# Value groups and reciprocals moved up in the image steps, and another order of loads ahead of the first expert tile

## Chip, cores and metric

The kernel runs on one core of a Trainium2 chip. The metric is the device time of one execution, in microseconds (us). Every run of the comparison uses the same inputs.

## What is computed

One layer of a small vision tower, all in float32, on 16 images of 128 tokens with 256 channels each:

```python
h = tok_mixer(x)                      # x: (16, 4, 128, 256); softmax-weighted sum over the 4 groups
h = h + attention(layernorm(h))       # 16 heads of 16, bias from relative positions, then Wo
h = h + moe(layernorm(h))             # 8 experts, top 2 of a softmax gate, 256 -> 1024 -> 256, exact GELU

# moe, as the reference has it
gates = softmax(x @ Wg + bg); mask = one_hot(top_k(gates, 2)); g = normalise(gates * mask)
eo = gelu(x @ W1[e] + b1[e]) @ W2[e] + b2[e];  out = sum_e g[e] * eo[e]
```

The kernel computes only the two chosen experts of a token. It sorts the 4096 (token, expert) pairs into 39 tiles of up to 128 rows with one expert each. The first 14 tiles (EARLY) are filled from images 0 to 10 alone, so that they can start before the last images are routed.

## The kernel before, in words

Each engine has its own program, written out by hand. The engines meet only at semaphores, and each runs its own instructions strictly in the written order.

**Image stage.** Step i of every engine's `step` works on three images at once: the front part does projections and scores of image i, the back part softmax sums, transposes, values and context of image i-1, and the late part output projection, residual, second norm and gate logits of image i-2. Steps 0 to 15 have a front; step 16 has only back and late. Steps 6, 10 and 13 also have gate work on VectorE (`gate_inputs`, `masks`, `gates`); steps 7, 11 and 14 have `ranks` on TensorE and `rows` on VectorE, which fix where the token records go.

- TensorE (lines 873 to 911): `project_qk`, `context` 0 and 1 (transposes of the probabilities, line 815), `out_project`, `project_v`, then `values(0)`, `context(2)`, `values(1)`, `scores(0)`, `context(3)`, `spread_sums` (transposes of the reciprocals, line 771), `values(2)`, `scores(1)`, `values(3)`, `turn_xn2`, `scores(2)`, `turn_x`, `scores(3)`, `gate_logits`. A `values` group is eight small matmuls (line 825) that use 32 of the array's columns each.
- VectorE (lines 1227 to 1265): token mixing of the next image (`select_groups`), `mask_keys` (line 263), `residual`, `first_norm` (line 1089, writes `xn1`), `rows`, `reciprocals` (line 1132), `spread` (two copies, line 1137), `second_norm` (line 1089, writes `xn2`), `masks`, `biased` 0 and 1 (line 1122: score plus bias and row minimum), `normalise`, `biased` 2 and 3.
- ScalarE (lines 605 to 634): copies out of PSUM and the exponentials (line 586), 16 per step in four groups. `exp(i, 0)` waits for `biased(i, 0)`; the last copies of a step are `x1T_evac` (line 555), which lets TensorE begin the next step, and `v_evac`.
- GpSimd (lines 447 to 456): the power -1/2 of the first norm (line 428), its half of `mask_keys` (line 263), the power of the second norm (line 428), and the scatters of token records into DRAM (line 439). Of these, a scatter with an even number waits until all scatters before it have landed.

**Hand-over.** After step 14 VectorE makes the table of the early tiles (`tile_table`, semaphore `tables_ok`). SyncE, which issues nearly all plain DMAs through one queue, has in order: seven times `load_w2(e)` (1 MB of second-layer weights, which waits until the images that lie in its place are used up) with `store_xn2` of two images (normed tokens and residual, 128 KB each), then `load_w2(7)`, a store of a padding row block, `b2` (result biases, 1 MB, line 324, waits for the last `biased`), a wait for `tables_ok`, a wait for the 22 early scatters (`scat`, line 327), then per tile the token records (`load_records`, `next_records`: 2 KB) and the first-layer matrix (`load_w1`: 1 MB). `next_records(j)` waits until the records of tile j-1 have landed.

**Expert stage.** GpSimd gathers the 128 token rows of a tile through its records (`gather`, line 476) and later scatter-adds the results (`scatter`, line 485). TensorE turns the rows (`turn_xs`, line 932), VectorE copies them out (`xs_evac`, line 1343), TensorE computes `hidden` (line 944, 32 matmuls), ScalarE applies GELU (line 672), and TensorE computes `second` (line 956) one tile behind. VectorE's `result` (line 1348) adds `b2`. Between the first two tiles TensorE has `out_project(15)` and VectorE `residual(15)`; before `xs_evac(0)` VectorE waits for `b2_in`.

## Time and profile before

| | |
|---|---|
| median of 3 runs | 566.88 us (564.5 to 567.76) |
| the profiled execution | 565.29 us, of which its span is 563.5 us |
| TensorE matmuls busy | 510.7 us (91% of the span) |
| VectorE busy | 239.5 us (42%) |
| ScalarE busy | 265.3 us (47%) |
| GpSimd busy | 200.2 us (36%) |
| mean granted TensorE clock | 0.976 of full speed |
| last chain, by engine | PE 60%, DVE 10%, issue 10%, DMA 8%, ACT 6%, POOL 3% |

PE is TensorE, DVE VectorE, ACT ScalarE, POOL GpSimd, SP SyncE. A busy share is a mean over stages that have different limits. The chain of work that ended last is followed back from the last instruction, at each step to what released it; "issue" is time in which an engine waited for nothing that the profile shows. The time in square brackets behind an instruction is how long its engine had been idle, with what ended that.

### The profile page before, as it was taken

How to read it: one execution, taken by the hardware profiler on the slowest of the kernel's cores; microseconds unless marked ns; L12 is line 12 of the kernel's file. 1: busy time of each engine (PE TensorE's matmuls, PEld its weight loads, DVE VectorE, ACT ScalarE, POOL GpSimd, SP SyncE). 2: the span in 40 equal slices, each digit the busy share in tenths (PEclk: the TensorE clock that was granted, in tenths of full speed). 3: DMA queues.
4: the chain of work that ended last, by engine and by line, in shares of the span. 5: the costliest groups of instructions: out<-in, count | busy, mean ns of one | idle time of the engine just before them, and what ended most of it. 6: DMA issues, size and time to landing. Idle time of an engine off the chain costs nothing.

```text
span 563.5 us, 13115 instructions
## 1 busy us (share of the span) xinstructions
PE 510.7 (91%) x3742; PEld 418.9 (74%) x3743; DVE 239.5 (42%) x1083; ACT 265.3 (47%) x1003; POOL 200.2 (36%) x186
## 2 busy tenths in 40 slices
PE   4789899999999989938999999999999999999980
PEld 3466666666666657617998999999999989999960
DVE  2777787888787887822233111111111111111110
ACT  1267688777887878743343333332233223333310
POOL 3041133334544455311326653333333333333221
PEclk9999899999999999978999999999999999999995
DMA  8890020303131221284566666666666666666615
GB/s 264 253 332 6 20 95 21 95 20 95 35 100 23 92 50 65 73 294 118 169 184 184 165 161 161 185 180 182 185 186 185 186 184 178 167 183 166 158 19 158
DMA packets 51004, 78.61 MB, mean 139 GB/s; under 512 B 10528, under 2 KB 39472, under 8 KB 50768
## 3 DMA queue, kind: packets, MB, share of 16 engines
q1 hardware_dynamic: 40160, 66.80, 36.6%
q0 software_dynamic: 8592, 10.58, 11.1%
q10 hardware_dynamic: 2208, 0.71, 0.6%
q8 instruction: 20, 0.33, 0.2%
q14 instruction: 24, 0.20, 0.1%
HBM read 68.27 MB, written 11.90 MB: 142 GB/s over the span
## 4 chain that ended last, share of the span: by engine, by line
PE 60%; DVE 10%; issue 10%; DMA 8%; ACT 6%; POOL 3%; POOLq 0%; SPq 0%; DVEq 0%; ACTq 0%
PE psVO L956 20%; PE psS L944 10%; PE psP L944 10%; ACT prob L586 5%; DMA fold<-xn_dram,sel 5%; PE psQK L782 4%; PE psS L805 3%; DVE prob L1122 3%; PE psP L815 3%; PE psVO L793 2%; PE psVO L836 2%; PE psQK L932 2%; DMA meta_dram<-meta,pos 1%; DMA sel<-meta_dram 1%; DVE st L1080 1%
## 5 line engine op out<-in xcount | busy, mean ns | idle before, releaser
L956 PE MATMUL psVO<-xw,prob 128*128 x624 | 142.0, 380 | 0.8 <-DVE fold L1348 0.8
L956 PEld LDWEIGHTS psVO<-xw,prob 128*128 128x128 f32 x624 | 115.5, 190 | 16.0 <-issue 1.2
L485 POOL DMA_INDIRECT sum_dram<-fold,sel x39 | 62.0, 1590 | 166.8 <-DMA sel<-meta_dram 125.2
L586 ACT ACTIVATE prob<-prob,smin 128x128 f32<-128x128 f32 x256 | 99.5, 395 | 15.0 <-DVE smin L1122 14.8
L672 ACT ACTIVATE prob<-psS,b1T 128x128 f32<-128x128 f32 x160 | 45.6, 368 | 99.6 <-PE psS L944 99.5
L672 ACT ACTIVATE prob<-psP,b1T 128x128 f32<-128x128 f32 x152 | 43.3, 368 | 95.6 <-PE psP L944 95.6
L428 POOL TENSOR_TENSOR rstd<-ve,minus_half 128x1 f32<-128x1 f32 x32 | 33.2, 1037 | 144.9 <-DVE ve L1085 139.2
L944 PEld LDWEIGHTS psS<-fold,w1c 128*128 128x128 f32 x640 | 75.8, 195 | 1.9 <-DVE fold L1343 1.0
L944 PE MATMUL psS<-fold,w1c 128*128 128x128 f32 x640 | 76.3, 278 | 0.6 <-DVE fold L1343 0.6
L944 PEld LDWEIGHTS psP<-fold,w1c 128*128 128x128 f32 x608 | 70.7, 192 | 3.0 <-DVE fold L1343 2.1
L944 PE MATMUL psP<-fold,w1c 128*128 128x128 f32 x608 | 71.1, 275 | 1.9 <-DVE fold L1343 1.9
L805 PE MATMUL psS<-kbd,qkT 128*128 128x512 f32 x128 | 68.5, 620 | 4.3 <-DVE kbd L263 2.9
L1348 DVE TENSOR_TENSOR fold<-psVO,relb 128x256 f32<-128x256 f32 x39 | 16.6, 425 | 122.4 <-PE psVO L956 122.4
L1122 DVE CUSTOM_DVE_ANT_0 prob<-psS,relb 128x128 f32<-128x128 f32 x256 | 59.0, 287 | 18.9 <-PE psS L805 15.6
L1343 DVE COPY fold<-psQK 128x256 f32<-128x256 f32 x39 | 16.5, 424 | 110.3 <-PE psQK L932 110.3
L575 ACT COPY pT<-psP 128x512 f32<-128x512 f32 x64 | 36.0, 591 | 30.5 <-PE psP L815 30.5
L586 ACT ACTIVATION_READ_ACCUMULATOR prob<-prob,smin 128x1 f32 x256 | 49.3, 193 | 0.0
L476 POOL DMA_INDIRECT fold<-xn_dram,sel x39 | 38.9, 998 | 21.3 <-issue 10.9
L782 PE MATMUL psQK<-x1T,wT 128*128 128x128 f32 x256 | 34.4, 290 | 6.0 <-ACT x1T L555 6.0
L815 PEld LDWEIGHTS psP<-ident,prob 128*128 128x128 f32 x256 | 29.3, 142 | 12.1 <-issue 11.1
L815 PE MATMUL psP<-ident,prob 128*128 128x128 f32 x256 | 37.0, 277 | 0.6 <-ACT prob L586 0.6
L782 PEld LDWEIGHTS psQK<-x1T,wT 128*128 128x128 f32 x256 | 31.3, 200 | 7.7 <-ACT x1T L555 7.4
(165 smaller groups left out, 535.6 us busy)
## 6 DMA issues: line engine op xcount, KB each, us to landing
w1c<-in_L_ffn_W SPq DMA_DIRECT2D x39, 1024.0 KB, 6.7
xw<-in_x SPq DMA_DIRECT2D x16, 512.0 KB, 8.1
xw<-in_L_ffn_W SPq DMA_DIRECT2D x8, 1024.0 KB, 6.7
sum_dram<-h_all SPq DMA_DIRECT2D x17, 128.0 KB, 2.5
xn_dram<-xn SPq DMA_DIRECT2D x16, 128.0 KB, 1.7
out<-sum_dram SPq DMA_DIRECT2D x4, 512.0 KB, 5.6
relb<-in_L_ffn_b SPq DMA_DIRECT2D x1, 1024.0 KB, 6.7
sel<-meta_dram SPq DMA_DIRECT2D x39, 2.0 KB
```

The lines of the kernel that those rows point to most:

```text
L428: pool.tensor_tensor(rstd[i][:, :], ve[i][:, :], minus_half[:, :], ALU.pow) \
L476: pool.indirect_dma_start(out=xs[j % 2], out_offset=None, in_=xn_dram.ap()[0:EARLY_B * S if j < EARLY else N_TOK, :], in_offset=bass.Indir ...
L485: pool.indirect_dma_start(out=sum_dram.ap()[0:EARLY_B * S if j < EARLY else N_TOK + P, :], out_offset=bass.IndirectOffsetOnAxis(ap=row_no[ ...
L575: act.copy(pT[c % 2][:, :], psP[c % 2][:, :]).then_inc(pT_sb, 1)
L586: i = act.activation(blk, blk, ACT.Exp, bias=smin[:, k:k + 1], scale=-1.0, accum_out=ssum[:, k:k + 1])
L672: i = act.activation(hT[u][:, c * P:(c + 1) * P], hidden_ps[u][c // 4][:, c % 4 * P:(c % 4 + 1) * P], ACT.Gelu, bias=b1T[:, bass.ds(e * HC ...
L782: i = pe.matmul(psQK[:, (t * DC + oc) * S:(t * DC + oc + 1) * S], wT[t][:, ic * D + oc * P:ic * D + oc * P + P], x1T[:, ic * S:(ic + 1) * ...
L805: pe.matmul(psS[c % 2][:, :], qkT[:, w * S:(w + 1) * S], kbd[:, c * CH * S:(c + 1) * CH * S], start=True, stop=True).then_inc(s_ps, 1)
L815: i = pe.transpose(psP[c % 2][:, n * S:(n + 1) * S], pr[:, h * S:(h + 1) * S], ident[:, :])
L944: i = pe.matmul(hidden_ps[u][c // 4][:, c % 4 * P:(c % 4 + 1) * P], w1c[u][:, d * H + c * P:d * H + (c + 1) * P], xsT[:, d * P:(d + 1) * P ...
L956: i = pe.matmul(psVO[:, 0:D], hT[u][:, c * P:(c + 1) * P], xw2[:, bass.ds(e * (HC * D) + c * D, D)], start=(c == 0), stop=(c == HC - 1))
L1122: i = dve.tensor_tensor_reduce(prob[u % 2][:, h * S:(h + 1) * S], psS[c % 2][:, n * S:(n + 1) * S], relb[:, h * S:(h + 1) * S], 1.0, HIGHE ...
```

## The change

Three pieces. (1) TensorE's step now has `values(0)` and `values(1)` together ahead of `context(2)`, and `values(2)` and `values(3)` together behind `scores(1)`. VectorE's step has `reciprocals` and `spread` ahead of `first_norm` and `rows`. (2) SyncE issues `load_w2(7)` after the store of image 12 instead of after that of image 13; then, as soon as the table is made, the first two first-layer matrices; then the store of image 13, the padding block, the wait for the scatters, the records of tiles 0 and 1, and only then `b2`. (3) In the first tiles TensorE has `turn_xs(1)` ahead of `out_project(15)`, and VectorE `xs_evac(1)` ahead of `residual(15)`; VectorE waits for `b2_in` just ahead of its first `result`.

```diff
--- before.py
+++ after.py
@@ -314,18 +314,6 @@
                 sp.dma_start(w2_e[:, bass.ds(e, 1)], W2[bass.ds(e, 1)].rearrange(
                     "e (c p) d -> p e c d", p=P)).then_inc(w2_in, 16)
 
-            with sp.Fori(0, E - 1) as e:
-                load_w2(e)
-                for u in range(2):
-                    store_xn2(2 * e + u)
-            load_w2(E - 1)
-            sp.dma_start(sum_dram.ap()[N_TOK:N_TOK + P, :], hcol(0)).then_inc(h_out, 16)
-            sp.wait_ge(s_min, NCH * B)
-            sp.dma_start(relb[:, 0:E * D], b2.rearrange("e d -> (e d)").partition_broadcast(P)) \
-                .then_inc(b2_in, 16)
-            sp.wait_ge(tables_ok, 1)
-            sp.wait_ge(scat, 16 * TOPK * EARLY_B)
-
             def load_records(j):
                 row = sp.value_load(tile_row[0:1, bass.ds(j, 1)], min_val=0, max_val=E * REGION)
                 sp.dma_start(metas[:, bass.ds(j * META, META)],
@@ -344,10 +332,24 @@
                 sp.dma_start(metas[:, bass.ds(j * META, META)],
                              meta_dram.ap()[bass.ds(row, P), :]).then_inc(metas_in, 16)
 
+            with sp.Fori(0, E - 2) as e:
+                load_w2(e)
+                for u in range(2):
+                    store_xn2(2 * e + u)
+            load_w2(E - 2)
+            store_xn2(B - 4)
+            load_w2(E - 1)
+            sp.wait_ge(tables_ok, 1)
+            load_w1(0, 0)
+            load_w1(1, 1)
+            store_xn2(B - 3)
+            sp.dma_start(sum_dram.ap()[N_TOK:N_TOK + P, :], hcol(0)).then_inc(h_out, 16)
+            sp.wait_ge(scat, 16 * TOPK * EARLY_B)
             load_records(0)
-            load_w1(0, 0)
             next_records(1)
-            load_w1(1, 1)
+            sp.wait_ge(s_min, NCH * B)
+            sp.dma_start(relb[:, 0:E * D], b2.rearrange("e d -> (e d)").partition_broadcast(P)) \
+                .then_inc(b2_in, 16)
             next_records(2)
             store_xn2(B - 2)
             next_records(3)
@@ -887,17 +889,17 @@
                     ranks(batch, i - 2)
                 if back:
                     values(i - 1, 0)
+                    values(i - 1, 1)
                     context(i - 1, 1 - u, 2)
-                    values(i - 1, 1)
                 if front:
                     scores(i, 0)
                 if back:
                     context(i - 1, 1 - u, 3)
                     spread_sums(i - 1)
-                    values(i - 1, 2)
                 if front:
                     scores(i, 1)
                 if back:
+                    values(i - 1, 2)
                     values(i - 1, 3)
                 if late:
                     turn_xn2(i - 2, batch)
@@ -973,8 +975,8 @@
             pe.wait_ge(r_sb, B)
             turn_xs(0, 0, 0)
             hidden(0, 0, 0)
+            turn_xs(1, 1, 0)
             out_project(B - 1)
-            turn_xs(1, 1, 0)
             tile(1, 1, 0)
             turn_xn2(B - 1, None)
             tile(2, 0, 1)
@@ -1237,14 +1239,13 @@
                     mask_keys(dve, i, 0)
                 if late:
                     residual(i - 2)
+                if back:
+                    reciprocals(i - 1, 1 - u)
+                    spread(i - 1)
                 if nxt:
                     first_norm(i + 1)
                 if place is not None:
                     rows(place)
-                if back:
-                    reciprocals(i - 1, 1 - u)
-                if back:
-                    spread(i - 1)
                 if late:
                     second_norm(i - 2)
                 if gate is not None:
@@ -1356,16 +1357,16 @@
                 return dve.value_load(tile_e[0:1, bass.ds(j, 1)], min_val=0, max_val=E - 1)
 
             dve.wait_ge(tables_ok, 1)
-            dve.wait_ge(b2_in, 16)
 
             last = len(BATCHES) - 1
             xs_evac(0)
             top_two(B - 2, slot(B - 2))
-            residual(B - 1)
             top_index(B - 2, slot(B - 2))
             xs_evac(1)
+            residual(B - 1)
             second_norm(B - 1)
             xs_evac(2)
+            dve.wait_ge(b2_in, 16)
             result(0, expert(0))
             xs_evac(3)
             result(1, expert(1))
```

## Rows read from the trace of the kernel before

**Rows 1.** Busy by stretch: PE, PEld, DVE, ACT, POOL; then PEclk, DMA share, GB/s.

```profile
66.00:238.00 172.00, 164.26 (x1206) 110.66 (x1205) 139.99 (x728) 135.40 (x548) 72.36 (x60) 0.99 0.21 60
...
238.00:254.00 16.00, 6.41 (x60) 3.78 (x58) 4.68 (x26) 7.58 (x26) 2.55 (x3) 0.77 0.80 290
...
254.00:563.00 309.00, 289.66 (x1972) 270.79 (x1972) 53.77 (x155) 92.08 (x316) 109.22 (x87) 0.97 0.60 166
```

**Rows 2.** Chain that ended last, 228 to 262 us: start, length, what.

```profile
227.64 1.66 DVE tile_e L1318
...
233.53 0.35 PE psCX L825 x8
...
234.64 7.00 DMA meta_dram<-meta,pos
...
242.68 2.71 DMA sel<-meta_dram
...
246.29 6.23 DMA fold<-xn_dram,sel
...
254.04 5.24 PE psS L944 x32
```

**Rows 3.** SyncE's queue in order of time: start, length, what; image 12 and eighth W2.

```profile
220.44 0.34 SPq L310 DMA_DIRECT2D sum_dram<-h_all  x1
...
234.91 0.41 SPq L314 DMA_DIRECT2D xw<-in_L_ffn_W  x1
```

**Rows 4.** Instructions of GpSimd in order of time, steps 14 and 16.

```profile
223.42 0.95 POOL L439 DMA_INDIRECT meta_dram<-meta,pos  x1 [1.40 <-DMA meta_dram<-meta,pos]
...
241.36 0.57 POOL L428 TENSOR_TENSOR rstd<-ve,minus_half 128x1 f32<-128x1 f32 x1 [5.73 <-issue]
```

**Rows 5.** DMA queues in 254 to 257 us: packets, MB, share of 16 engines.

```profile
q0 software_dynamic: 46, 0.13, 14.6%
```

**Rows 6.** Chain that ended last, 296 to 322 us: a gather beside one matrix load.

```profile
299.95 4.93 DMA fold<-xn_dram,sel
```

**Rows 7.** TensorE in order of time, last image step: two value groups together, last matmuls.

```profile
243.50 0.70 PE L825 MATMUL psCX<-pT,v_s 128*32 128x128 f32 x16
...
244.13 0.44 PE L851 MATMUL psG<-ident,xn 128*128 128x128 f32 x2
...
245.03 0.61 PE L857 MATMUL psG<-wg_s,x2T 128*128 128x8 f32 x4 [0.46 <-ACT x2T L603]
```

**Rows 8.** Busy time and granted clock just after TensorE stopped.

```profile
246.00:248.00 2.00, 0.00 (x0) 0.00 (x0) 0.41 (x3) 0.48 (x2) 1.02 (x1) 0.69 1.02 414
```

**Rows 9.** TensorE in order of time, hidden layer of the second tile.

```profile
262.21 3.84 PE L944 MATMUL psP<-fold,w1c 128*128 128x128 f32 x32 [1.85 <-DVE fold L1343]
```

**Rows 10.** All engines in order of time, a plain image step (144 to 160 us).

```profile
148.62 1.50 POOL L428 TENSOR_TENSOR rstd<-ve,minus_half 128x1 f32<-128x1 f32 x1 [6.20 <-DVE ve L1085]
...
151.46 0.68 DVE L1089 TENSOR_SCALAR xn<-h_all,mv,rstd 128x256 f32<-128x256 f32 x1
...
151.96 0.65 POOL L428 TENSOR_TENSOR rstd<-ve,minus_half 128x1 f32<-128x1 f32 x1
...
152.74 0.41 DVE L1089 TENSOR_SCALAR xn<-h_all,mv,rstd 128x256 f32<-128x256 f32 x1
...
154.14 0.40 ACT L586 ACTIVATE prob<-prob,smin 128x128 f32<-128x128 f32 x1 [0.53 <-DVE smin L1122]
```

**Rows 11.** VectorE and ScalarE in order of time, step 11 (a step with ranks).

```profile
181.80 0.29 DVE L1122 CUSTOM_DVE_ANT_0 prob<-psS,relb 128x128 f32<-128x128 f32 x1 [1.11 <-PE psS L805]
...
183.11 0.40 ACT L586 ACTIVATE prob<-prob,smin 128x128 f32<-128x128 f32 x1 [0.37 <-DVE smin L1122]
```

**Rows 12.** All engines in order of time, step 2 (54 to 65 us).

```profile
59.03 0.44 PE L771 MATMUL psQK<-ident,srcw 128*128 128x128 f32 x2 [0.91 <-DVE srcw L1137]
...
61.06 0.29 DVE L1122 CUSTOM_DVE_ANT_0 prob<-psS,relb 128x128 f32<-128x128 f32 x1 [0.90 <-PE psS L805]
```

**Rows 13.** Line 1137, the copies of `spread`: count, ns min/median/max, shape.

```profile
L1137 DVE COPY srcw<-srcp x32: 218/224/228, 43.0 to 242.9; 128x128 f32<-128x128 f32 x32
```

## What the change was predicted to do

> **What bounds the kernel now.** I read the busy time by stretch first, then the chain that ended last through the hand-over, then the order of time of each engine around it, and last one plain and two special image steps.
>
> The stretches [rows 1] show three stages. From 66 to 238 us (image stage) TensorE's matmuls are busy for 164.26 of 172 us, but VectorE and ScalarE are busy for some 140 and 135 us too: no engine alone bounds it. From 254 us on (experts) TensorE is busy for 289.66 of 309 us and VectorE for 53.77: TensorE bounds it, so what the hand-over gains or loses arrives at the end unchanged. Between them, 238 to 254 us, TensorE is busy for 6.41 of 16 us.
>
> The chain [rows 2] says what it waited for: the last early record scatter took 7.00 us to land (234.64 to 241.64), the first records 2.71 us, GpSimd's start 0.9 us, the gather 6.23 us (246.29 to 252.52), then turn, copy, and the first hidden layer at 254.04. The scatter was slow in company: 0.27 us after it SyncE issued the 1 MB of `load_w2(7)` [rows 3]. A pair of such scatters in step 14, with no big load beside it, had landed by 223.42, 2.4 us after the second was issued at 221.04 [rows 4].
>
> **Part 1: the loads.** `load_w2(7)` moves from 234.91 to just behind the store of image 12 at 220.44 [rows 3], so to 221.0. The two W1 loads can start when the table is made, 0.3 us behind the end of line 1318 at 229.3 [rows 2], so at some 230.5 and 231.6, and are done before the gather. `b2` comes behind the records of tile 1.
>
> The scatter now meets 2 MB of W1, which should have passed by some 237, and three 128 KB stores, instead of W2 and stores. But W2 now lies beside the second scatter of step 14's first pair. If that one takes 7.00 us as its like did [rows 2], GpSimd's next two scatters go at 228 instead of 223.42 [rows 4], their landing meets W1, and the last two scatters of step 15, which wait for them, go late as well: between 233.3 (as now) and 237. Their last landing is thus at 237.0 (2.4 us as in the undisturbed pair) at best, and at worst at 241.6, as now. I take 239.0, between the two, since the W1 queue is empty by then. From landing to gather is 4.65 us today [rows 2], which gives 243.6; GpSimd's own floor is the end of its power of image 14, 241.93 [rows 4], which is earlier.
>
> The gather itself: beside nothing its 0.13 MB had moved by 257, 2.8 us after its issue at 254.22 [rows 5]; beside one matrix load it took 4.93 us in the chain [rows 6]; beside two, 6.23. It now has `b2` beside it, one load of 1 MB, issued just before it. I take 4.4. It lands at 248.0 instead of 252.5: **4.5 us** sooner. Bounds: 242.2 + 2.8 = 245.0, which TensorE can use only from 245.64, the end of its gate logits [rows 7], so 6.9 us; and 246.3 + 4.9 = 251.2, so 1.3 us.
>
> The clock: TensorE stopped at 245.64, and its granted clock fell from 1.00 to 0.50 within 246 to 248, where the mean is 0.69 [rows 8], so about 1.5 us after. The first hidden layer ran partly at 0.50 and took 5.24 us [rows 2], the second, at full clock, 3.84 [rows 9]. With a landing at 248.0 the gap is still 2.4 us, so I count no gain here; the bound is 1.4 us for a gap that ends in time.
>
> The three 128 KB stores, the padding block among them, fall behind W1 in the queue. Who waits for a landed store is `second_norm` of image 14 in step 16, behind the power at 241.36 [rows 4], and W1 is through by 237: nothing. SyncE's wait for the table (229.6) stands ahead of the store of image 13, which comes one step behind that at 220.44: nothing. The `b2` wait on VectorE now stands ahead of `result(0)`, some 10 us after `b2` should land: nothing.
>
> **Part 2: the order in the first tiles.** The second hidden layer waited 1.85 us for VectorE's copy [rows 9], which stood behind the residual and statistics of image 15. With `turn_xs(1)` ahead of `out_project(15)` the copy runs beside that projection, and with it ahead of `residual(15)` nothing is in front of it. For the first tile, from the gather's landing through turn and copy to the hidden layer, it took 1.5 us at half clock [rows 2]; turn and projection fill about 1.1 of it here, at full clock. I take nearly the whole wait, **1.8 us** (at least 1.4). Image 15's norm is now later by one copy, 0.4 us, and its reader, `turn_xn2(15)`, has a whole tile of slack.
>
> **Part 3: the image steps.** On TensorE two value groups together take 0.63 us from start to start [rows 7], while one alone takes 0.35 [rows 2] and costs its neighbours a little more; I put the whole at 0.5 us a step, and `scores(1)` also starts one group (0.35) sooner. What that is worth depends on the step.
>
> In a plain step [rows 10] it is worth nothing. ScalarE's exponentials begin at 154.14 when VectorE's `biased(0)` is ready, and from there ScalarE runs without a gap to the copy that lets TensorE begin again. `biased(0)` stands behind `second_norm` at 152.74, and that behind GpSimd's power, 151.96 + 0.65 = 152.61. The new order on VectorE is the same four pieces; it can't pass 152.61. So zero for nine of the twelve steps 3 to 14.
>
> In steps 7, 11 and 14 `rows` makes VectorE late, and the second group of scores too: `biased(1)` waited 1.11 us for TensorE, and ScalarE 0.37 us for it [rows 11]. `first_norm` no longer begins inside GpSimd's `mask_keys`, where it takes 0.68 instead of 0.41 us [rows 10]. I take 0.3 us each, **0.9** together (0.3 to 1.8).
>
> In step 2 TensorE waited 0.91 us for `spread`, and `biased(1)` 0.90 us for TensorE [rows 12]; behind `biased(2)` and `(3)` stands the token mixing weights' work, for which everything waits. I take 0.75 us; in step 1, where TensorE is the bound, the 0.5 of above. Together **1.3** (0.5 to 1.9).
>
> In step 15 VectorE's table instruction of line 1318 took 1.66 us [rows 2] for 14 numbers, beside GpSimd's `mask_keys`. If GpSimd is late there, as in part 1, it doesn't collide: 0.3 us, between 0 and 1.4.
>
> The lock that shows in these rows has a rule in the Trainium skill, SBUF — State Buffer, "Who interferes with whom": copies and tensor_scalar with a fast two-port mode share a port pair with GpSimd, and the loser blocks for the whole instruction. By it the two copies of `spread`, now beside `mask_keys`, would block too, which is rival B below. The rows bear out `first_norm`, and show nothing of the copies, which at 224 ns [rows 13] never stood beside `mask_keys`.
>
> **The sum.** 4.5 + 1.8 + 0.9 + 1.3 + 0.3 = 8.8 us. Against the profiled execution, 565.29 us (span 563.5 and 1.8 around it): 556.5. Its time is 1.6 us below the median of the three runs; I allow for half of that: **557.3 us**.
>
> **Rivals.**
>
> A: the gather lands early. The scatters aren't held up by W1, land at 237.0, and the gather goes at its floor. For it: the pair of step 14 [rows 4]. Against it: 7.00 and 6.23 us [rows 2]. Price: 6.9 instead of 4.5, and the clock doesn't fall, 1.4: 3.8 more, 553.5 us. The Trainium skill speaks for this one (DMA: Bandwidth & Descriptors, "Queues, rings and completion order"): each DMA engine takes turns between the queues, packet by packet.
>
> B: the port. `spread`'s two copies and `first_norm` stand in a row just where GpSimd's power wants the port. The power could lose up to 0.45 us a step, and `second_norm` waits for it. Against it: in step 15 both ran side by side. Twelve steps by 0.35: 4.2 us back, 561.5.
>
> C: the records stay late. GpSimd's scatters of steps 14 and 15 queue up behind W2 and W1, and the landing is at 241.6 as before: 3.2 of the 4.5 are gone, 560.5. This is also the case in which the change doesn't do what it says: the matrices come first, but the records bound.
>
> D: slower. The same place as B at its worst: GpSimd's power waits behind both copies and `first_norm` (0.2 + 0.2 + 0.4 us), and is then as slow as it is beside VectorE's `mask_keys`, 1.50 us instead of 0.65 [rows 10]. That is up to 1.65 us in each of the thirteen steps 2 to 14; it decides from 0.68 us a step on (8.8 by 13). At 1.1 us, two thirds of its worst, it costs 14.3: 571.6 us.
>
> **How the numbers follow.** Forecast 0.55 (its own range 555 to 559.5), A 0.15, B 0.14, C 0.12, D 0.04. The range holds forecast, A, B and most of C: 553.0 to 563.0. A measurement tells about 0.5% from no change, here 2.8 us: faster is below 564.0, which holds forecast, A, and nearly all of B and C: 0.92. Same 0.05, from B and C together; slower 0.03, from D.
>
> **What would show it.** In the trace after: the last record scatter lands near 239; the gather is issued near 243.6 less the image stage's gain and takes 4 to 5 us; the idle before the second hidden layer is below 0.2 us; the plain steps (4, 5, 8, 9) keep their length; `xn2` starts no later behind GpSimd's power than now; line 1318 is short. If plain steps grow, B or D; if the scatter lands at 241 or later, C; if the clock stays at 1.00, A. It would be wrong altogether if some other wait, such as GpSimd's second half of the keys in step 15, held TensorE up.

## The result, and the profile after

The changed kernel takes 557.14 us (median of 4 runs, 556.79 to 558.64), the kernel before beside it 566.38 us (4 runs, 564.5 to 567.76). The ratio is 0.9857, with a 95% interval from 0.9828 to 0.9885, so 8.1 us gained by the ratio (6.5 to 9.7; the two medians differ by 9.2). The profiled execution took 557.38 us with a span of 555.6 (before: 563.5), at a mean granted clock of 0.981.

Busy time of the changed kernel by stretch; columns as in [rows 1]:

```profile
66.00:238.00 172.00, 155.76 (x1206) 109.62 (x1204) 135.40 (x734) 136.15 (x553) 72.53 (x60) 1.00 0.27 77
238.00:254.00 16.00, 9.26 (x71) 6.87 (x70) 3.98 (x18) 6.48 (x21) 3.50 (x4) 0.81 0.35 112
254.00:563.00 309.00, 285.36 (x1955) 267.51 (x1953) 53.66 (x152) 91.83 (x316) 108.26 (x86) 0.98 0.60 166
```

TensorE is busy for 9.26 us of the hand-over's 16 instead of 6.41. In the image stage it is busy for 8.5 us less, and the stage did not become shorter by that much. Of the 8.5 us, 5.2 are the value groups (22.1 us before, 16.9 in pairs); what TensorE saved it mostly waited instead, for the copy that lets it begin a step (5.6 us before, 13.7 after). Its chain of waits through the hand-over, beside [rows 2]:

```profile
233.21 5.86 DMA meta_dram<-meta,pos
...
239.80 1.63 DMA sel<-meta_dram
...
242.33 5.99 DMA fold<-xn_dram,sel
248.32 0.24 issue
248.56 0.68 PE psQK L934 x2
...
249.84 6.24 PE psS L946 x32
```

The scatter landed at 239.07 (241.64 before), the gather at 248.32 (252.52). The gather still took 5.99 us, and the first hidden layer behind it takes 6.24 us instead of 5.24. TensorE in order of time then:

```profile
244.09 0.61 PE L859 MATMUL psG<-wg_s,x2T 128*128 128x8 f32 x4 [0.86 <-ACT x2T L605]
248.56 0.66 PE L934 MATMUL psQK<-ident,fold 128*128 128x128 f32 x2 [3.86 <-DMA fold<-xn_dram,sel]
...
257.00 3.73 PE L946 MATMUL psP<-fold,w1c 128*128 128x128 f32 x32
```

The second hidden layer has no bracket: the 1.85 us of [rows 9] are gone. Granted clock just after TensorE stopped, where [rows 8] stood at 0.69 in the first 2 us:

```profile
246.00:248.00 2.00, 0.00 (x0) 0.00 (x0) 0.00 (x0) 0.00 (x0) 0.00 (x0) 1.00 0.91 282
248.00:250.00 2.00, 0.82 (x3) 0.45 (x3) 0.61 (x4) 0.00 (x0) 0.00 (x0) 0.52 0.24 80
...
252.00:254.00 2.00, 2.00 (x11) 2.00 (x11) 0.00 (x0) 0.23 (x1) 0.00 (x0) 0.50 0.08 29
254.00:256.00 2.00, 2.00 (x16) 2.00 (x15) 0.00 (x0) 0.91 (x4) 0.00 (x0) 0.78 0.00 0
```

The clock was at 0.50 from 248.1 to 254.9 us, over 5.1 of the first layer's 6.24 us. In the kernel before it was at 0.50 from 246.8 to 257.0, but the layer began only at 254.04, so that 3.0 of its 5.24 us lay there. In a second profile of the changed kernel the clock had fallen already at 245.7, 0.3 us after TensorE stopped:

```profile
244.00:246.00 2.00, 0.68 (x5) 0.52 (x4) 0.97 (x5) 1.68 (x3) 0.90 (x1) 0.92 0.99 319
246.00:248.00 2.00, 0.00 (x0) 0.00 (x0) 0.15 (x1) 0.18 (x1) 0.07 (x1) 0.50 0.98 277
...
254.00:256.00 2.00, 2.00 (x12) 2.00 (x11) 0.00 (x0) 1.14 (x4) 0.00 (x0) 0.53 0.00 0
```

It came back at 255.9, and the first layer, from 250.45 on, took 6.42 us. So the layer is longer in both profiles of the changed kernel, whenever the clock fell: it begins earlier, and in both the full clock was back no sooner than 6.3 us after the turn (4.2 us in the kernel before).

How far the changed kernel is ahead at the same piece of work, from the two traces: 0.94 us at the end of the gate logits of image 14, 4.20 at the first turn (252.76 and 248.56), 5.21 at the second hidden layer (262.21 and 257.00), 7.1 at the last `second` of a full order (543.80 and 536.70), 7.9 at the end. The two executions did not start level: the changed kernel began step 1 of the images 0.57 us later (36.98 against 36.41 us), and in the other profiles that start lies between 36.1 and 37.7. Counted from step 1, where nothing of the change has acted yet, the leads are 0.57 us larger: 1.5 at the gate logits, 4.8 at the first turn, 5.8 at the second hidden layer. The forecast had 2.5, then 7.0, then 8.8, and nothing after that. The end is right within a microsecond, the places are not; the runs below say why.

### The profile page after: what moved, and what is told of

It is laid out like the page before. It is cut to its first block, busy times and chain, and to the rows that moved or that the text cites. A ratio compares the mean times of both kernels' runs of the same rounds, so it can differ in the third digit from the quotient of the medians.

```text
span 555.6 us, 13098 instructions
## 1 busy us (share of the span) xinstructions
PE 501.0 (90%) x3742; PEld 418.6 (75%) x3743; DVE 233.6 (42%) x1083; ACT 264.9 (48%) x1003; POOL 200.3 (36%) x186
## 4 chain that ended last, share of the span: by engine, by line
PE 53%; issue 26%; POOL 9%; DMA 5%; DVE 2%; ACT 2%; POOLq 0%; DVEq 0%; SPq 0%; ACTq 0%
PE psVO L958 22%; PE psS L946 12%; PE psP L946 12%; POOL kbd L263 3%; DMA fold<-xn_dram,sel 3%; POOL meta_dram L441 3%; ACT prob L588 2%; POOL rstd L430 2%; PE psQK L934 2%; PE psQK L784 1%; DMA meta_dram<-meta,pos 1%; PE psP L817 1%; PE psVO L838 1%; DMA sum_dram<-fold,sel 1%; PE psVO L795 1%
## 5 line engine op out<-in xcount | busy, mean ns | idle before, releaser
L807 PE MATMUL psS<-kbd,qkT 128*128 128x512 f32 x128 | 65.9, 599 | 3.4 <-DVE smin L1124 1.9
L1124 DVE CUSTOM_DVE_ANT_0 prob<-psS,relb 128x128 f32<-128x128 f32 x256 | 57.6, 286 | 7.1 <-PE psS L807 5.6
L784 PE MATMUL psQK<-x1T,wT 128*128 128x128 f32 x256 | 32.8, 281 | 14.1 <-ACT x1T L557 14.1
L784 PEld LDWEIGHTS psQK<-x1T,wT 128*128 128x128 f32 x256 | 29.8, 191 | 15.9 <-ACT x1T L557 15.5
L441 POOL DMA_INDIRECT meta_dram<-meta,pos x32 | 31.8, 994 | 17.7 <-DMA meta_dram<-meta,pos 6.4
```

The costliest lines, as they stand in the source:

```text
L441: pool.indirect_dma_start(out=meta_dram.ap()[:, :], out_offset=bass.IndirectOffsetOnAxis(ap=pos[:, i:i + 1], axis=0), in_=meta[:, i * META ...
L784: i = pe.matmul(psQK[:, (t * DC + oc) * S:(t * DC + oc + 1) * S], wT[t][:, ic * D + oc * P:ic * D + oc * P + P], x1T[:, ic * S:(ic + 1) * ...
L807: pe.matmul(psS[c % 2][:, :], qkT[:, w * S:(w + 1) * S], kbd[:, c * CH * S:(c + 1) * CH * S], start=True, stop=True).then_inc(s_ps, 1)
L1124: i = dve.tensor_tensor_reduce(prob[u % 2][:, h * S:(h + 1) * S], psS[c % 2][:, n * S:(n + 1) * S], relb[:, h * S:(h + 1) * S], 1.0, HIGHE ...
```

## Experiments

All times are medians; the ratio to the kernel before, run beside it on the same chip, is what compares kernels. The kernel before was at 565.19 us beside the first four, 566.15 beside the next four, 564.71 beside the last four.

### Each part alone

The loads (part 1, with VectorE's `b2_in` wait moved), against the kernel before:

```diff
+            store_xn2(B - 4)
+            load_w2(E - 1)
+            sp.wait_ge(tables_ok, 1)
+            load_w1(0, 0)
+            load_w1(1, 1)
+            store_xn2(B - 3)
...
```

> Kernel before with SyncE's new order of loads and the b2 wait ahead of the first result; image steps and first tiles as before. Prediction's terms: 4.5 us for the gather and 0.3 for line 1318, so 4.8 us faster than before. Rival (the trace of the changed kernel): the gather lands 4.2 us sooner, but the hidden layer of the first tile pays 1.0 us more for the clock, line 1318 gives about 1 us, and the expert stage runs without its small waits for gathers (1.8 us): 6 us faster. Both: the idle of 1.85 us before the second hidden layer is still there.

Measured: 562.7 us, ratio 0.9953 (0.9933 to 0.9974), so 2.7 us gained, less than both the term (4.8) and the rival (6). GpSimd's scatters and first gather in this run:

```profile
228.53 0.96 POOL L441 DMA_INDIRECT meta_dram<-meta,pos  x1 [5.67 <-DMA meta_dram<-meta,pos]
...
237.50 1.03 POOL L441 DMA_INDIRECT meta_dram<-meta,pos  x1 [4.04 <-DMA meta_dram<-meta,pos]
238.84 0.98 POOL L441 DMA_INDIRECT meta_dram<-meta,pos  x1 [0.30 <-issue]
244.25 1.02 POOL L478 DMA_INDIRECT fold<-xn_dram,sel  x1 [1.95 <-DMA sel<-meta_dram]
```

W2 beside the first pair of step 14 holds the second pair until 228.53 (before: 223.42 [rows 4]), as forecast (228); W1 beside that one holds the last pair until 237.50, half a microsecond past the latest I had allowed (this execution began its step 1 0.74 us later than the one of the kernel before). The last scatter then took only 2.13 us, and the gather, with `b2` beside it, 5.94. This is rival C's mechanism, in part: matrices first, records late.

The order in the first tiles (part 2):

```diff
+            turn_xs(1, 1, 0)
             out_project(B - 1)
-            turn_xs(1, 1, 0)
...
-            residual(B - 1)
             top_index(B - 2, slot(B - 2))
             xs_evac(1)
+            residual(B - 1)
```

> Kernel before with only turn_xs(1) ahead of out_project(15) and xs_evac(1) ahead of residual(15). Prediction's term: 1.8 us faster than before, the idle of 1.85 us before the second hidden layer gone, nothing else moved. Rival: image 15's norm is later and takes part of it back in the tiles after it, less than 1.0 us faster.

Measured: 563.51 us, ratio 0.9964 (0.9949 to 0.9979), 2.0 us gained. Forecast: 1.8. In its trace the second hidden layer starts 6.17 us behind the first instead of 8.17.

The image steps (part 3):

```diff
                     values(i - 1, 0)
+                    values(i - 1, 1)
                     context(i - 1, 1 - u, 2)
-                    values(i - 1, 1)
...
-                    values(i - 1, 2)
                 if front:
                     scores(i, 1)
                 if back:
+                    values(i - 1, 2)
                     values(i - 1, 3)
...
+                if back:
+                    reciprocals(i - 1, 1 - u)
+                    spread(i - 1)
                 if nxt:
                     first_norm(i + 1)
```

> Kernel before with only the new orders in the image steps of TensorE and VectorE. Prediction's terms: 1.3 us in steps 1 and 2, 0.9 in steps 7, 11 and 14, together 2.2 us faster than before. Rival (the trace of the changed kernel): 0.9 to 1.0 us are gained by step 4, but steps 7, 11 and 14 each grow, by 0.2 to 0.6 us, because the last value group and the turn of xn2 end about a microsecond later than in the kernel before; together between 0.5 us faster and 0.5 us slower. If the growth came from the new loads it would be absent here.

Measured: 560.41 us, ratio 0.9918 (0.9891 to 0.9945), 4.6 us gained, where I had 2.2 (2.5 with line 1318). In its trace the gains stand where they were forecast but are larger: 1.5 us by the start of step 3 (forecast 1.3), 0.5, 0.7 and 0.3 us in steps 7, 11 and 14 (forecast 0.9 for the three), 0.65 in step 15 (forecast 0.3), so 3.9 at the gate logits. The plain steps keep their length. At the first turn it is 5.1 us: the scatter and the gather ride along, and the gather took 5.50 instead of 6.23 us.

Loads and tiles together, the steps as before:

> Changed kernel with the image steps of TensorE and VectorE as before: the loads and the order of the first tiles. Prediction's terms: 4.5 + 1.8 + 0.3 = 6.6 us faster than before. Rival: the steps give nothing or take something, so this is as fast as the whole change or faster, 8 to 9.5 us faster than before.

Measured: 560.0 us, ratio 0.9919 (0.9891 to 0.9948), 4.6 us: the sum of the two alone (4.7), below the term (6.6) and far from the rival (8 to 9.5). The three parts alone add to 9.3 us; the whole has 8.1, and 7.0 when it was measured again (below). With intervals of 0.9 to 1.7 us to either side of each of these, the times alone don't show that the parts lose by being together; the traces do.

### The steps in the whole

> The changed kernel once more, unaltered, as the measure for the runs beside it. Its first profile had the place steps 7, 11 and 14 longer than in the kernel before (14.07, 14.00 and 13.88 us), while the run with the new step orders alone had each of them shorter by 0.3 to 0.7 us. In the long ones VectorE's normalise and ScalarE's copy of x2T were both released 0.7 to 1.3 us late, together. Theory: TensorE loses this time in every execution once loads and steps are combined; then the growth is here again and the time is 557.1 us. Rival: a property of the one profiled execution; then steps 7, 11 and 14 are at 13.0 to 13.3 us here, the gate logits of image 14 end some 2.5 us sooner than in the first profile, and the profiled execution has 555 to 556 us.

Measured: 559.29 us, ratio 0.9877 (0.9847 to 0.9908), 7.0 us gained; its interval and the first one overlap. The second profile shows the same growth (14.07, 13.93 and 13.89 us), so the theory holds for the steps: they are long in both profiles. The time expected, 557.1 us, was missed by 2.2. This is what the growth looks like in step 11, in TensorE, VectorE and ScalarE of the changed kernel (first profile):

```profile
180.03 0.64 PE L827 MATMUL psCX<-pT,v_s 128*32 128x128 f32 x16
180.61 0.44 PE L853 MATMUL psG<-ident,xn 128*128 128x128 f32 x2
...
182.38 0.42 DVE L1150 TENSOR_TENSOR ctxT<-psCX,rT 128x256 f32<-128x256 f32 x1 [0.90 <-remote]
...
182.42 0.37 ACT L605 COPY x2T<-psG 128x256 f32<-128x256 f32 x1 [0.83 <-PE psG L853]
```

The same of the run with the steps alone:

```profile
178.44 0.65 PE L825 MATMUL psCX<-pT,v_s 128*32 128x128 f32 x16
179.01 0.44 PE L851 MATMUL psG<-ident,xn 128*128 128x128 f32 x2
...
179.81 0.42 DVE L1148 TENSOR_TENSOR ctxT<-psCX,rT 128x256 f32<-128x256 f32 x1
...
179.91 0.35 ACT L603 COPY x2T<-psG 128x256 f32<-128x256 f32 x1
```

TensorE's rows start at the same distances, but VectorE's `normalise` follows the value pair by 2.35 us instead of 1.37, and ScalarE's copy follows the turn by 1.8 instead of 0.9. I call this the late completion. In a plain step it is hidden, in the three steps with ranks and rows it costs 0.85 to 1.05 us each: 14.07, 14.00 and 13.88 us against 13.02, 13.06 and 13.03. Some of this comes back in step 15: from the start of step 1 to the end of the last gate logits the changed kernel takes 2.3 us more than the run with the steps alone.

One half of the steps' change undone, TensorE's:

```diff
-                    values(i - 1, 1)
                     context(i - 1, 1 - u, 2)
+                    values(i - 1, 1)
...
+                    values(i - 1, 2)
                 if front:
                     scores(i, 1)
                 if back:
-                    values(i - 1, 2)
```

> The changed kernel with TensorE's old order in the image steps (value groups 0 and 1 and groups 2 and 3 apart), VectorE's new order kept. The step orders together brought 4.6 to 4.8 us alone and 2.9 us on top of the other two parts. Theory V, VectorE's half carries it (spread sooner takes away TensorE's wait in step 2 and in the place steps): 557.1 to 557.9 us, place steps as short as in the run with both orders. Theory P, TensorE's half carries it (paired groups cost 0.2 us less in each step and the second group of scores begins 0.35 us sooner): 559.0 to 560.0, near the 560.0 of the kernel with both old orders.

and VectorE's:

```diff
-                if back:
-                    reciprocals(i - 1, 1 - u)
-                    spread(i - 1)
...
                     rows(place)
+                if back:
+                    reciprocals(i - 1, 1 - u)
+                if back:
+                    spread(i - 1)
```

> The changed kernel with VectorE's old order in the image steps (first_norm and rows ahead of reciprocals and spread), TensorE's new order kept. Theory V: 559.3 to 560.0 us; step 2 keeps TensorE's wait of 0.9 us for spread. Theory P: 557.1 to 557.9. If both halves are needed at once, this and its counterpart are both near 559 to 560.

Measured: 559.26 us (ratio 0.9893, 0.9864 to 0.9922) and 558.88 us (0.9884, 0.9858 to 0.991), beside 559.29 of the whole. The two theories aren't told apart: each half alone does as well as both within the intervals, and the late completion is in all three (in steps 7, 11 and 14 `normalise` starts 1.4 to 1.6 us behind the last value group with TensorE's old order, 1.9 to 2.1 with VectorE's old, 2.3 to 2.5 with both new; 1.1 to 1.4 with both old). From the start of step 1 to that of step 3, where it is absent, the halves are plain: 0.5 us from VectorE's order, 1.0 from TensorE's, 1.5 from both.

Which other part brings the late completion? The whole without part 2, as below, and the whole without part 1 (SyncE's program and the `b2_in` wait of the kernel before):

```diff
+            out_project(B - 1)
             turn_xs(1, 1, 0)
-            out_project(B - 1)
...
+            residual(B - 1)
             top_index(B - 2, slot(B - 2))
             xs_evac(1)
-            residual(B - 1)
```

> The changed kernel without part 2 (the old order in the first expert tiles). The three parts alone gave 2.6, 2.0 and 4.7 us, 9.3 together, and the whole 8.1 and 7.0 in two comparisons. In every kernel with moved loads and the new step orders together the completions of TensorE's last value groups reach VectorE and ScalarE some 1 us later than in the run with the new step orders alone, where VectorE's normalise starts 1.1 us behind the start of the last group. If the loads' part brings this: it is here too, steps 7, 11 and 14 are 13.8 to 14.1 us long, the time is 559 to 560 (its parts alone would give 558.7). If the order of the first tiles brings it: steps 7, 11 and 14 are at 12.9 to 13.3 us and the time is 558 to 558.7.

> The changed kernel without part 1 (the old order of loads). Its two parts alone would give 6.7 us, so 559.3 against 566. If the order of the first tiles brings the late completions of TensorE's value groups: steps 7, 11 and 14 are 13.8 to 14.1 us long here and the time is 560 to 561. If the loads' part brings them: these steps are at 12.9 to 13.3 us, and the time is 559 to 559.5. If they are in neither of this and its counterpart, only all three together have them, and it is a matter of how the programs lie in memory rather than of what any of them does.

Measured: 556.86 us (0.9879, 0.9849 to 0.9909) and 558.69 us (0.991, 0.9883 to 0.9937). Neither has it; steps 7, 11 and 14 are at 13.0 to 13.1 us in both. So neither pair of parts brings it; all three parts together had it here. But three parts together need not: the kernel with W2 moved once more (below) has all of them and the same instructions as the one with `b2` late (below), with two SyncE pieces in the other order from 211 us on. The one with `b2` late has the late completion from 129 us on, the other never. So the work of the engines up to there is not what makes it. The instruction queues carried the same packets in both (8 and 12 from 66 to 210 us). That the programs lie differently in memory, the third case put down ahead, was not tested: what makes it is open.

The times show what it hides. Without part 2 the kernel gains 6.8 us, which can't be told from the 8.1 and 7.0 of the whole, though part 2 alone is worth 2.0.

### The gather, the records and the clock

`b2` behind the records of tile 3:

```diff
             next_records(1)
-            sp.wait_ge(s_min, NCH * B)
-            sp.dma_start(relb[:, 0:E * D], b2.rearrange("e d -> (e d)").partition_broadcast(P)) \
-                .then_inc(b2_in, 16)
             next_records(2)
             store_xn2(B - 2)
             next_records(3)
+            sp.wait_ge(s_min, NCH * B)
+            sp.dma_start(relb[:, 0:E * D], b2.rearrange("e d -> (e d)").partition_broadcast(P)) \
+                .then_inc(b2_in, 16)
```

> The changed kernel with the load of the result biases (1 MB, written to all partitions) behind the records of tile 3, so that it is not beside the first gather. In the changed kernel the gather took 5.99 us where I had put 4.4, and in the run with the loads alone about as much. Theory: b2 is what slows it; it takes 3.0 to 4.4 us here, lands at 245.5 to 246.7, and the time is 555.5 us, or 554 if TensorE's clock is kept, since TensorE stopped at 244.7. Rival: the gather is that slow beside its own kind, the three 128 KB stores and the second gather; it still takes 5.5 to 6 us, and the time is 557.1.

Measured: 555.03 us (550.94 to 557.41), ratio 0.9802 (0.9763 to 0.9842), against 0.9877 of the changed kernel beside it: 4.2 us more gained. GpSimd, then TensorE:

```profile
242.02 1.02 POOL L478 DMA_INDIRECT fold<-xn_dram,sel  x1 [2.22 <-DMA sel<-meta_dram]
```

```profile
242.91 0.61 PE L859 MATMUL psG<-wg_s,x2T 128*128 128x8 f32 x4 [0.46 <-ACT x2T L605]
245.04 0.41 PE L934 MATMUL psQK<-ident,fold 128*128 128x128 f32 x2 [1.51 <-DMA fold<-xn_dram,sel]
246.06 5.47 PE L946 MATMUL psS<-fold,w1c 128*128 128x128 f32 x32 [0.61 <-DVE fold L1344]
```

From 242.02 to the turn at 245.04 are 3.0 us, and some 0.24 of them lie between landing and turn, as in the chain above: the gather took 2.8 us, not 6.0. `b2` was the 3.2 us, and the floor of the prediction, 2.8 [rows 5], was exact. In the seven profiles with `b2` just ahead of it the first gather took 5.5 to 6.1 us; in the four with the two W1 loads around it, as in the kernel before, 5.5 to 6.2. The clock was not kept, though TensorE stood for 1.5 us only, but it was low for a shorter time (246.6 to 250.0), and the first layer took 5.47 us instead of 6.24: 0.8 us more of the 4.2.

W2 one place up as well:

```diff
             load_w2(E - 2)
+            load_w2(E - 1)
             store_xn2(B - 4)
-            load_w2(E - 1)
```

> The changed kernel with two loads moved once more: the result biases behind the records of tile 3, as in the run before, and the last W2 matrix one place up, ahead of the stores of image 12, so that it starts when image 15's tokens are summed (212.6 us) and is through by some 218, before the scatters of step 14. There, W2 beside the first pair of scatters held the second pair up to 225.4 to 228.5 (before the change 223.4), and in two of the four profiles that hold-up reached the last pair of step 15 (235.0 to 235.1 instead of 231 to 232). Theory: W2's place decides whether the last records are late. Then the second pair goes at 222 to 223.5, the last pair never waits for it (231 to 232), and the time is 552.5 to 554 us against 555.0 with b2 late alone, with less spread between executions. Rival: the last scatter's 6 us beside the two W1 loads bounds it alone; then the second pair is early, the last landing is still at 238.8 or later and the time stays at 555 us.

Measured: 550.12 us (549.46 to 551.95), ratio 0.9746 (0.9726 to 0.9766), so 14.3 us gained, more than forecast, and with less spread than with `b2` late alone, as forecast. It beats both kernels, the changed one by 1.1 to 1.3% by the ratios. GpSimd, VectorE and TensorE:

```profile
221.32 0.95 POOL L441 DMA_INDIRECT meta_dram<-meta,pos  x1 [1.40 <-DMA meta_dram<-meta,pos]
...
229.84 1.03 POOL L441 DMA_INDIRECT meta_dram<-meta,pos  x1 [0.21 <-issue]
...
239.53 1.02 POOL L478 DMA_INDIRECT fold<-xn_dram,sel  x1 [1.08 <-DMA sel<-meta_dram]
```

```profile
242.98 0.15 DVE L1332 TENSOR_TENSOR fold<-fold 1x8 f32<-1x8 f32 x1
243.17 0.42 DVE L1344 COPY fold<-psQK 128x256 f32<-128x256 f32 x1
```

```profile
242.58 0.41 PE L934 MATMUL psQK<-ident,fold 128*128 128x128 f32 x2 [0.41 <-DMA fold<-xn_dram,sel]
243.65 5.46 PE L946 MATMUL psS<-fold,w1c 128*128 128x128 f32 x32 [0.66 <-DVE fold L1344]
```

The second pair goes at 221.32, undisturbed, and the last pair waits for GpSimd's power alone. TensorE turns 0.4 us after the last gate logits, and the copy to xs starts right behind `tiles_taken`, VectorE's small instructions that prepare the late table (lines 1329 to 1332). In the chain that ended last there is no DMA between 226 and 250 us. By these profiles little of the further gain is W2's place. This kernel starts step 1 0.67 us later than the one with `b2` late, starts step 15 2.15 us ahead of it, which is the late completion that it doesn't have (2.8 us in steps 7, 11 and 14), and is 2.46 us ahead at the first turn. That leaves 0.3 us for W2 in these two profiles; no run has W2's place without the other difference.

Then TensorE kept at work between logits and turn:

```diff
             pe.wait_ge(r_sb, B)
+            pe.wait_ge(ctx_ok, B)
+            for n in range(8):
+                pe.matmul(psCX[:, 0:DC * S], ident[:, :], wT[0][:, 0:DC * S], start=True, stop=True)
             turn_xs(0, 0, 0)
```

> The kernel of the run above with eight matrix products added that nobody reads (256 columns each, some 2 us together) between the gate logits of image 14 and turn_xs of tile 0, so that TensorE doesn't stop at 243.5. With b2 late TensorE stood only from 243.9 to 245.0, and its granted clock still fell at 246.6 and stayed at 0.50 until 250, so that the first hidden layer took 6.2 to 6.4 us where the second takes 3.8. Theory: the pause is what costs the clock; without it the clock stays at 1.00, the first hidden layer takes 3.7 to 4 us, the products delay the turn by at most 0.7, and the time is 1.5 to 2 us below the kernel without them. Rival: the low share of TensorE's busy time from 238 on costs the clock, not the pause alone; it falls all the same, and the time is the same or up to 0.7 us longer.

Measured: 551.96 us, ratio 0.978 (0.9762 to 0.9799), 1.8 us slower than without. TensorE, and the granted clock in the 2 us from 244 and from 246, in this run:

```profile
241.21 3.70 PE L978 MATMUL psCX<-wT,ident 128*128 128x256 f32 x16
244.74 0.38 PE L934 MATMUL psQK<-ident,fold 128*128 128x128 f32 x2
245.74 3.84 PE L946 MATMUL psS<-fold,w1c 128*128 128x128 f32 x32 [0.61 <-DVE fold L1347]
```

```profile
244.00:246.00 2.00, 1.39 (x9) 0.99 (x8) 0.71 (x4) 0.00 (x0) 0.08 (x1) 1.00 0.54 109
246.00:248.00 2.00, 2.00 (x20) 2.00 (x20) 0.03 (x1) 0.06 (x1) 0.88 (x1) 1.00 1.01 420
```

and in the run without the products:

```profile
244.00:246.00 2.00, 2.00 (x15) 2.00 (x13) 0.00 (x0) 0.00 (x0) 0.74 (x1) 0.64 0.76 230
246.00:248.00 2.00, 2.00 (x11) 2.00 (x11) 0.00 (x0) 1.14 (x4) 0.00 (x0) 0.51 0.93 385
```

(The 6.2 to 6.4 us in the expectation are the changed kernel's; with `b2` late the first layer took 5.47.) With the products the clock stays at 1.00, and the first hidden layer takes 3.84 us; from first to second layer it takes 4.76 us instead of 6.39, so the clock is worth 1.6 us here. But I had mis-sized them: 3.70 us, not 2 (each product is two passes of 0.23 us), which put the turn off to 3.4 us behind the logits instead of 0.4. So neither the theory's time nor the rival's came.

In the run without them TensorE stood for 0.4 and 0.7 us, and the clock fell all the same, at 244.6. From 240 to 244 us it had been busy for 2.5 of 4 us, with the products for 3.5. At the start of step 15 the kernel with `b2` late stood for 1.19 us, behind steps in which TensorE is nearly always busy, and its clock stayed at 1.00. So the length of the pause alone does not decide. What does, these runs don't separate: the products fill the pause and the time ahead of it at once. Two products, which would fit the gap, were not tried.

## Why the prediction held, point by point

**The sum held by offsetting errors.** Loads and steps were to bring 7.0 us at the first turn and brought 4.2 (4.8 counted from step 1); the first tiles 1.8 and brought 1.0 there; the experts nothing and brought 2.7. That 557.14 lies 0.2 us from 557.3 is luck: the same kernel had 559.29 beside the later runs.

**Part 1.** The landing was put at 239.0 and is at 239.07 (239.7 in the second profile). That is luck too: 239.0 was the middle between a best and a worst case. In the first profile the last pair was not held up, and its second scatter took 5.86 us from 233.21; in the second it was held up to 235.10, and its second scatter took 3.26 us from 236.43. The records took 1.63 us, not 2.71, so the gather went at 242.33 instead of 243.6. The step that failed is its length: 4.4 taken, 5.99 measured. I had scaled by the number of loads beside it; the runs show 5.5 to 6.1 with `b2` issued just ahead and 2.8 without. The bounds (2.8 and 4.9) left the true value out. The part alone gave 2.7 of 4.8 us with its line 1318, since there the records were late as well.

**The clock.** I counted no gain, with a gain as the only bound; it became a loss of 1.0 us (6.24 instead of 5.24; 6.42 in the second profile). The layer came 4.2 us earlier, but the full clock only 2.1 us earlier (254.9 instead of 257.0), and in the second profile 1.1 us earlier. When the clock fell did not decide it: 3.4 us after TensorE stopped in one profile, 0.3 us in the other (in the kernel before 1.1 us, which I had read as 1.5). That the sum had its bound on one side only was the mistake: the step that is missing is how long the clock stays low once work is back.

**Part 2.** The wait of 1.85 us is gone, and alone the part is worth 2.0. In the whole 1.0 more arrives at the second layer than at the first, which is 2.0 less the clock's 1.0.

**Part 3.** The mechanism was right in each place, the sizes too small: 3.9 against 2.5 by the gate logits. In steps 7, 11 and 14 I had taken 0.3 each, between 0.1 and 0.6; measured 0.5, 0.7 and 0.3. In step 2 TensorE still waits 0.76 us for `spread` (0.91 before), for the reason given under the rivals; the gain there, 0.8 us, is that of both orders. Line 1318 is short, as forecast, and in the run with the steps alone for another reason than the late GpSimd I had named: VectorE passes it at 223.83 in 0.16 us, 0.34 us ahead of GpSimd's `mask_keys` (before: 1.66 us, begun 0.26 us behind the start of `mask_keys`). In the whole the late completion took 2.8 back in steps 7, 11 and 14, which nobody could read from the trace of before. Plain steps keep 12.6 us, as forecast.

**After the hand-over.** In the kernel before TensorE's turns waited for gathers four more times, in the changed kernel never. From the list of who waited for whom, TensorE of the kernel before, 262 to 563 us (us in total, times, longest):

```profile
PE psQK L932 <- DMA fold<-xn_dram,sel: 1.2, 4, 0.4
```

These 1.2 us are most of the growth of the lead from 5.2 to 7.1 us; the last 0.8 us, up to the end, were not traced. "What the hand-over gains arrives at the end unchanged" was thus too low: a gather that is early keeps the later ones early too.

**The rivals.** B and D asked for GpSimd's power to become slow. It takes 624 ns in the median of 32 after, 648 before:

```profile
L430 POOL TENSOR_TENSOR rstd<-ve,minus_half x32: 552/624/1621, 22.0 to 258.8; 128x1 f32<-128x1 f32 x32
```

What was held up is the first copy of `spread`. GpSimd and VectorE in step 2, then all 32 copies:

```profile
56.28 1.89 POOL L263 TENSOR_TENSOR kbd<-qkT,hmask 128x1024 f32<-128x1024 f32 x1
...
57.54 0.86 DVE L1139 COPY srcw<-srcp 128x128 f32<-128x128 f32 x2
...
58.13 0.62 POOL L430 TENSOR_TENSOR rstd<-ve,minus_half 128x1 f32<-128x1 f32 x1
```

```profile
L1139 DVE COPY srcw<-srcp x32: 213/224/785, 42.5 to 241.5; 128x128 f32<-128x128 f32 x32
```

In each of steps 1 to 14 the first copy begins inside `mask_keys`, 0.14 to 0.70 us ahead of its end. In step 6, where it is 0.14 us, the copy takes its usual 228 ns; in the others it takes 297 to 785 ns and ends 0.09 us after `mask_keys`. The second copy, beside GpSimd's power, takes 0.22 us as ever. The Trainium skill's rule (SBUF — State Buffer, "Who interferes with whom") says that whichever of the two engines issues first has the shared port pair for its whole instruction and the other blocks. The trace agrees, and it bears out what the prediction took from the rule for the copies; only the power, for which B and D feared, was spared.

A had the Trainium skill behind it (DMA: Bandwidth & Descriptors, "Queues, rings and completion order"), by which each DMA engine takes turns between the queues, packet by packet. Whatever the turns were, they did not spare the gather here: beside `b2` its 0.13 MB took 3.2 us longer. How long a turn lasted no run here shows, so the rule is neither borne out nor refuted.

C is real (228.53 and 237.50 above), but in the whole it cost little, since the landing hardly moved, as said under part 1.

## What to carry to other kernels

Here a small transfer on the critical path was slow when a large one had been issued just ahead of it, on another queue: moving `b2` by four DMA issues brought 4.2 us, more than each of the three parts but one. That is worth looking for in any chain that holds small DMAs. Move a big load to where nothing small follows for as long as it takes to drain, not merely earlier. And two profiles should be compared from a point that the change can't have reached, since they may not start level. A forecast whose parts ride on one another (a scatter that follows the steps, a clock that follows the gap) should bound each in both directions, even where its sum looks safe.

## What was not expected of the hardware

- The completions of TensorE's value groups reached VectorE and ScalarE some 1 us later in some kernels than in others with the same TensorE and VectorE programs up to that point (2.35 against 1.37 us in step 11), the same in both profiles of the changed kernel, and with nothing in the rows of TensorE to show it. The cause is open; it costs 2.8 us in steps 7, 11 and 14.
- One load of 1 MB ahead of a gather of 0.13 MB lengthens it from 2.8 to 6.0 us, as much as two did (6.23).
- TensorE's granted clock fell to half (1.2 GHz) after a pause of 0.4 us behind a stretch with 2.5 of 4 us busy; with the gap filled by products it stayed at 1.00 (2.4 GHz). After full stops it fell 1.1 us on in the kernel before, and 3.4 and 0.3 us on in two profiles of the same changed kernel.
- A VectorE copy of 0.22 us took up to 0.79 us when it began inside GpSimd's `mask_keys`: it ended 0.09 us after it.
